# Spreading the small VectorE operations of a segment softmax between the large ones of a graph-attention loop

## The reference, cut to what matters

```python
Q, K, V = ((enh @ W + b).reshape(N, 4, 64) for W, b in ...)      # N = 3125 nodes, 4 heads
mod_k = K[src] + 0.2 * rel_w[edge_relations][:, None, :]
scores = einsum('ehd,ehd->eh', Q[dst], mod_k) / 8
seg_max = segment_max(scores, dst)
ex = exp(scores - seg_max[dst]); w = ex / segment_sum(ex, dst)[dst]
agg = segment_sum(w[:, :, None] * V[src], dst)
```

## Time and profile before

| | us |
|---|---|
| median of 3 runs | 1417.63 (1417.37 to 1419.28) |
| the profiled execution | 1413.7 |
| its span, first to last instruction | 1411.7 |
| iterations 2 to 28 of `phase_edges` | 249.44 to 898.64, 649.20 |
| iterations 29 and 30 | 898.64 to 939.32, 40.68 |
| one chunk, from the first one-hots (L735) of a step 2 to the next chunk's, 502.21 to 526.24 | 24.03 |
| mean granted TensorE clock | 0.929 |

### The profile page before, as it was taken

How to read it: one execution, slowest core, us unless ns; L and a number is a source line. 1 busy time by engine, 2 the same in 40 slices (tenths; PEclk the granted TensorE clock), 3 DMA queues, 4 the chain that set the end, 5 groups by cost and what they waited for, 6 DMA issues and landing times. The chain is left out here.

```text
span 1411.7 us, 26741 instructions
## 1 busy us (share of the span) xinstructions
PE 1120.5 (79%) x7285; PEld 865.7 (61%) x7286; DVE 968.9 (69%) x2208; ACT 824.8 (58%) x2932; POOL 739.4 (52%) x853
## 2 busy tenths in 40 slices
PE   6999746888888888888888888756676479999950
PEld 4777533666666666666666666536565269999950
DVE  7676238999999999999999999634663832112115
ACT  3444300777878787878777777852244047767730
POOL 4666267766666666666666666005321444555520
PEclk9999966899999999999999999989995689999985
DMA  8232458877777777777777777038001722222218
GB/s 230 96 119 95 107 152 253 235 225 210 217 210 213 214 209 216 207 214 209 216 208 216 211 216 213 18 119 274 19 19 56 233 75 70 67 67 67 70 38 272
DMA packets 132711, 225.07 MB, mean 159 GB/s; under 512 B 23555, under 2 KB 89098, under 8 KB 132594
## 3 DMA queue, kind: packets, MB, share of 16 engines
q0 software_dynamic: 43456, 138.49, 34.9%
q1 hardware_dynamic: 89138, 85.16, 20.0%
HBM read 191.18 MB, written 32.40 MB: 158 GB/s over the span
## 5 line engine op out<-in xcount | busy, mean ns | idle before, releaser
L568 POOL DMA_INDIRECT KV<-kv,ixs x464 | 456.9, 985 | 227.1 <-issue 115.1
L583 ACT ACTIVATE KV<-KV,WS 128x65 f32<-128x65 f32 x1856 | 469.7, 337 | 19.3 <-ACT RR L609 17.0
L669 PE MATMUL ps_o<-KV,PM 128*128 128x260 f32 x928 | 254.4, 397 | 18.7 <-DVE PM L764 8.5
L653 PE MATMUL ps_qe<-Q,PT 128*128 x1392 | 200.0, 283 | 3.9 <-DVE KV L753 3.9
L669 PEld LDWEIGHTS ps_o<-KV,PM 128*128 128x128 f32 x928 | 159.6, 192 | 64.8 <-issue 30.0
L653 PEld LDWEIGHTS ps_qe<-Q,PT 128*128 128x128 bf16 x1392 | 139.3, 101 | 53.8 <-issue 7.0
L675 PE MATMUL ps_o<-ACC,ident 128*128 x464 | 154.8, 416 | 0.0
L753 DVE TENSOR_TENSOR KV<-KV,ps_qe 128x512 f32<-128x512 f32 x232 | 147.6, 673 | 0.8 <-PE ps_qe L653 0.5
L759 DVE TENSOR_REDUCE S<-KV 128x16 f32<-128x1024 f32 x116 | 141.5, 1220 | 7.6 <-DVEq L815 0.5
L746 DVE TENSOR_TENSOR KV<-KV,ps_u 128x1024 f32<-128x1024 f32 x116 | 139.8, 1205 | 3.9 <-DMA KV<-kv,ixs 3.9
L1434 DVE TENSOR_TENSOR YG<-ps_y,B 128x256 f32<-128x256 f32 x56 | 23.8, 425 | 170.0 <-PE ps_y L1408 170.0
(11 more groups left out here) (299 smaller groups left out, 1670.8 us busy)
## 6 DMA issues: line engine op xcount, KB each, us to landing
dlb<-dl_rows SPq DMA_DIRECT2D x116, 128.0 KB
W<-in_f_W_dram SPq DMA_DIRECT2D x16, 512.0 KB, 6.0
tyb<-ty_rows SPq DMA_DIRECT2D x116, 64.0 KB
KV<-kv,ixs POOLq DMA_INDIRECT x464, 4.2
kv<-kvb SPq DMA_DIRECT2D x25, 258.0 KB, 2.6
xs_rows<-xs SPq DMA_DIRECT2D x25, 256.0 KB, 2.5
YF<-ytab SPq DMA_DIRECT2D x8, 640.0 KB, 9.2
VB<-kv SPq DMA_DIRECT2D x5, 650.0 KB, 9.0
```

Source lines behind the costliest of these rows:

```text
L568: pool.indirect_dma_start(kv[:, c % KR, n, :], None, d["kv"], bass.IndirectOffsetOnAxis(ap=T["ixs"][:, c % KR, n:n + 1], axis=0)).then_inc ...
L583: m = a.activation(part, part, ACT.Copy, scale=W[:, c % 2, s * H + h:s * H + h + 1])
L653: m = pe.matmul(T["ps_qe"][:, p % 3, k, :], T["PT"][:, h, (p % 2 * 2 + k) * P:(p % 2 * 2 + k + 1) * P], T["Q3"][:, bass.ds(at + n * C, C)] ...
L669: m = pe.matmul(T["ps_o"][:, p % 2, 0:A], PM[:, p % 2, k, :], kv[:, c % KR, 2 * x + k, C:KVW], start=(k == 0), stop=False)
```

## The change

- `softmax(c, g)` is taken apart into functions which stand at several places of the step, and `then` is gone. Each operation only counts up `s_sm`; a wait stands where a result is read. The trailing ENGINE_NOP of g = 3 goes, so `SMV` is 12 in place of 13.
- Order of a step of VectorE after: `onehots(G+1)`; g 3: `first_rows`; `modify`; g 2: `carry_in(0)`; g 3: `factors`; `place`; g 0: `run_forward`; g 2: `carry_in(1)`; `multiply`; g 2: `differences`; (last two chunks: `weigh(p + 1)`); `multiply`; g 0: `rescale`, `run_backward`; g 1: `carry`; `reduce`; g 1: `carried`.
- `place` makes the one-hots of a group in one operation, 128 x 512, in place of two of 128 x 256. `PM` has two buffers of a group. TensorE's `aggregate(p)` waits for the group's.
- For the last two chunks summed (pairs from `VP` on) the odd pair of each group is weighed by VectorE in one TENSOR_TENSOR of 128 x 2 x 4 x 65, the even one by ScalarE.
- ScalarE's `exponents` moves from the middle of step 3 to the end of step 2. TensorE's `turn_weights` moves from behind the last `aggregate` of step 3 to in front of it.

```diff
-    SMV = 13
+    SMV = 12
+    VP = (NCH - 2) * CP
+
+    def on_vector(p):
+        return p >= VP and p % 2 == 1
@@ scalar
-                        if g == 3:
-                            exponents(i - 1)
                     if i >= 2:
-                        weigh(p + 1)
+                        if not on_vector(p + 1):
+                            weigh(p + 1)
                         keep_sums(p, at[0])
                         before = at[1]
+                    if g == 2 and 1 <= i <= NCH:
+                        exponents(i - 1)
@@ tensor, aggregate
-                pe.wait_ge(s_pm, p + 1)
-                pe.wait_ge(s_wv, p + 1)
+                pe.wait_ge(s_pm, p // 2 + 1)
+                if on_vector(p):
+                    pe.wait_ge(s_wd, (p - VP) // 2 + 1)
+                else:
+                    pe.wait_ge(s_wv, p + 1 if p < VP else VP + (p - VP) // 2 + 1)
@@ tensor, loop
+                    if 1 <= i <= NCH and g == 3:
+                        turn_weights(i - 1)
                     if p >= 0:
                         aggregate(p + 1)
-                    if 1 <= i <= NCH and g == 3:
-                        turn_weights(i - 1)
@@ vector
             def place(p):
-                wait(v, s_pw, p - 1)
-                v.tensor_tensor(PM[:, p % 2, :, :], T["iota_f"][:, :].unsqueeze(1).broadcast_to([P, 2, P]),
-                                T["DC"][:, 2 * p:2 * p + 2].unsqueeze(2).broadcast_to([P, 2, P]), ALU.is_equal).then_inc(s_pm, 1)
+                wait(v, s_pw, p - 2)
+                v.tensor_tensor(PM[:, p // 2 % 2, :, :], T["iota_f"][:, :].unsqueeze(1).broadcast_to([P, G, P]),
+                                T["DC"][:, 2 * p:2 * p + G].unsqueeze(2).broadcast_to([P, G, P]), ALU.is_equal).then_inc(s_pm, 1)
+
+            def weigh(p):
+                c, x = divmod(p, CP)
+                v.wait_ge(s_w, 2 * c + 2)
+                part = kv[:, c % KR, 2 * x:2 * x + 2, C:KVW].rearrange("p s (h d) -> p s h d", h=H)
+                w = W[:, c % 2, 2 * x * H:(2 * x + 2) * H].rearrange("p (s h) -> p s h", h=H)
+                v.tensor_tensor(part, part, w.unsqueeze(3).broadcast_to([P, 2, H, D + 1]), ALU.mult).then_inc(s_wd, 1)
...
+            def run_forward(c):
+                br, et = chunk_rows(c)
+                v.wait_ge(s_bl[c % 2], 80 * (c // 2 + 1))
+                v.wait_ge(s_t1, c + 1)
+                v.tensor_tensor_scan(SF[:, :], br[:, 0, :], ps_s[0:B, 0:P], -BIG, ALU.add, ALU.max).then_inc(s_sm, 1)
+
+            def run_backward(c):
+                br, et = chunk_rows(c)
+                v.wait_ge(s_sm, c * SMV + 1)
+                wait(v, s_t2, c)
+                v.tensor_tensor_scan(SB[:, ::-1], br[:, 1, ::-1], SF[:, ::-1], -BIG, ALU.add, ALU.max).then_inc(s_sm, 1)
+
+            def carry(c):
+                br, et = chunk_rows(c)
+                v.wait_ge(s_ez, c + 1)
+                v.tensor_tensor_scan(line(ec[0:1, 0, :, :]), line(et[:, 0, :, :]), line(ez[0:1, 0, :, :]), -BIG, ALU.add, ALU.max).then_inc(s_sm, 1)
+                v.tensor_tensor_scan(line(ec[0:1, 1, :, :])[:, ::-1], line(et[:, 1, :, :])[:, ::-1], line(ez[0:1, 1, :, :])[:, ::-1], -BIG,
+                                     ALU.add, ALU.max).then_inc(s_sm, 1)
+
+            def carried(c):
+                br, et = chunk_rows(c)
+                v.wait_ge(s_sm, c * SMV + 4)
+                wait(v, s_t3, c)
+                v.tensor_copy(ez[0:1, 0, :, 0:1], ec[0:1, 0, :, CB_:CB_ + 1]).then_inc(s_sm, 1)
+                v.tensor_tensor(turned_line(cr[0:1, 0, :]), ec[0:1, 0, :, 0:CB_], et[:, 2, :, 1:CB_ + 1], ALU.add).then_inc(s_sm, 1)
+                v.tensor_tensor(turned_line(cr[0:1, 1, :]), ec[0:1, 1, :, 2:EW], et[:, 3, :, 1:CB_ + 1], ALU.add).then_inc(s_sm, 1)
+
+            def carry_in(c, n):
+                br, et = chunk_rows(c)
+                if n == 0:
                     v.wait_ge(s_t3, c + 1)
+                    v.wait_ge(s_sm, c * SMV + 7)
+                else:
+                    v.wait_ge(s_sm, c * SMV + 8)
+                v.scalar_tensor_tensor(out=SM[:, :], in0=br[:, 2 + n, :], scalar=ps_s[0:B, 256 + n:257 + n], in1=(SM if n else SB)[:, :],
+                                       op0=ALU.add, op1=ALU.max).then_inc(s_sm, 1)
+
+            def differences(c):
+                v.wait_ge(s_sm, c * SMV + 9)
+                wait(v, s_ex, c)
+                v.tensor_tensor(SD[0:H, P:P + 1], ps_s[0:H, 256:257], SM[0:H, 0:1], ALU.subtract).then_inc(s_sm, 1)
+                v.tensor_tensor(SD[:, 0:P], ps_s[0:B, 0:P], SM[:, :], ALU.subtract).then_inc(s_sm, 1)
+
+            def first_rows(c):
+                v.tensor_scalar(T["OH"][:, :], T["iota_f"][0:H, :], T["d0"][:, c:c + 1], None, ALU.is_equal).then_inc(s_sm, 1)
+
+            def factors(c):
+                v.wait_ge(s_sm, c * SMV + 12)
+                wait(v, s_t4, c)
+                v.wait_ge(s_ex, c + 1)
+                v.scalar_tensor_tensor(out=T["LR"][:, :], in0=T["OH"][:, :], scalar=T["SE"][0:H, P:P + 1], in1=T["OH"][:, :],
+                                       op0=ALU.mult, op1=ALU.subtract).then_inc(s_lr, 1)
@@ setup
-                          ... "PM": ((P, 2, 2, P), F32),
+                          ... "PM": ((P, 2, G, P), F32),
```

More of the change, by code:

```diff
@@ L517, in phase_edges @@
     s_bl = [sem(f"ed_breaks{h}") for h in range(2)]
-    (s_ix, s_oh, s_u, s_qe, s_ku, s_mu, s_sc, s_pm, s_wv, s_pw, s_o, s_acc, s_rs, s_ld) = (sem("ed_" + n) for n in
+    (s_ix, s_oh, s_u, s_qe, s_ku, s_mu, s_sc, s_pm, s_wv, s_pw, s_o, s_acc, s_rs, s_ld, s_wd) = (sem("ed_" + n) for n in
         ("indices", "onehots", "relations", "queries", "modified", "multiplied", "scores", "placements", "weighted", "placed", "products",
-         "added", "rescaled", "loads"))
+         "added", "rescaled", "loads", "weighted_by_vector"))
     (s_t1, s_t2, s_t3, s_t4, s_ez, s_sm, s_ex, s_lr, s_w) = (sem("sm_" + n) for n in
@@ L664, in aggregate @@
                 c, x = divmod(p, CP)
-                pe.wait_ge(s_pm, p + 1)
-                pe.wait_ge(s_wv, p + 1)
+                pe.wait_ge(s_pm, p // 2 + 1)
[3 more added lines that the diff above has]
+                    pe.wait_ge(s_wv, p + 1 if p < VP else VP + (p - VP) // 2 + 1)
                 wait(pe, s_acc, p - 1)
                 for k in range(2):
-                    m = pe.matmul(T["ps_o"][:, p % 2, 0:A], PM[:, p % 2, k, :], kv[:, c % KR, 2 * x + k, C:KVW], start=(k == 0), stop=False)
+                    m = pe.matmul(T["ps_o"][:, p % 2, 0:A], PM[:, p // 2 % 2, p % 2 * 2 + k, :], kv[:, c % KR, 2 * x + k, C:KVW], start=(k == 0), stop=False)
                 m.then_inc(s_pw, 1)
@@ L773, in rescale @@
                                        op0=ALU.add, op1=ALU.mult).then_inc(s_rs, 1)
[L775 to L801, removed]
-                    v.wait_ge(s_t3, c + 1)
[L803 to L815, removed]
@@ new lines, in _, with chunk_rows, line, turned_line @@
+            ez, ec, cr, SF, SB, SM, SD = (T[n] for n in ("EZ", "EC", "CR", "SF", "SB", "SM", "SD"))
+            def chunk_rows(c):
+                return T["BR"][:, c % 2, :, :], T["ET"][0:1, c % 2, :, :, :]
+            def line(t):
+                return t.rearrange("a h s -> a (h s)")
+            def turned_line(t):
+                return t.rearrange("a (s h) -> a h s", h=H)
+            def run_forward(c):
[3 more added lines that the diff above has]
+                v.tensor_tensor_scan(SF[:, :], br[:, 0, :], ps_s[0:B, 0:P], -BIG, ALU.add, ALU.max).then_inc(s_sm, 1)
@@ L821, in _ @@
                     p = (i - 2) * CP + 2 * g
+                    c = i - 1
+                    scored, softmax, summed = G_ < NG, 1 <= i <= NCH, i >= 2
                     if G_ + 1 < NG:
                         onehots(G_ + 1)
-                    if G_ < NG:
+                    if softmax and g == 3:
+                        first_rows(c)
+                    if scored:
                         modify(G_)
-                    if i >= 2:
-                        place(p)
-                        place(p + 1)
-                    if G_ < NG:
-                        multiply(2 * G_)
+                    if softmax and g == 2:
+                        carry_in(c, 0)
+                    if softmax and g == 3:
+                        factors(c)
+                    if summed:
+                        place(p)
+                    if softmax and g == 0:
+                        run_forward(c)
+                    if softmax and g == 2:
+                        carry_in(c, 1)
+                    if scored:
+                        multiply(2 * G_)
+                    if softmax and g == 2:
+                        differences(c)
+                    if summed and on_vector(p + 1):
+                        weigh(p + 1)
+                    if scored:
                         multiply(2 * G_ + 1)
-                    if i >= 2 and g == 0:
+                    if summed and g == 0:
                         rescale(i - 2)
-                    if 1 <= i <= NCH:
```

(11 more changed lines are left out.)

## The result

The changed kernel takes **1360.21 us** (median of 4, 1357.18 to 1360.95) against 1417.5 before; ratio 0.9595, 95% interval 0.9571 to 0.9618. Forecast 1357.6. The profiled execution has a span of 1359.1 against 1411.7, 52.6 less.

| stretch, us | before | after | difference | forecast |
|---|---|---|---|---|
| up to the end of iteration 1 | 249.41 | 250.43 | +1.0 | -1 |
| iterations 2 to 28 | 648.92 | 596.01 | -52.9 | -54.8 |
| iterations 29 and 30 | 40.99 | 37.97 | -3.0 | -4.2 |
| all behind | 472.4 | 474.7 | +2.3 | 0 |

A forecast was written before the change was run, and what follows sets the result against it. VectorE, 96% busy in iterations 2 to 28, was taken as the bound. 1413.7 - 54.8 (27 chunks) - 1 (iteration 1) - 4.2 (end) = 1353.7 profiled, 1357.6 against the median; own range 1350 to 1369, 8 in 10: 1349 to 1375.

The forecast's parts named there:

- The price of a wait: VectorE's softmax: a wait for the instruction just issued costs 0.11 to 0.12 us; twelve removed save 1.32 a chunk.
- The NOP's 0.22: VectorE, behind `LR`: removing the ENGINE_NOP brings `reduce` from 0.48 to 0.26 after `LR` starts, 0.22 us a chunk.
- The rule that I had priced as a rival: VectorE: next operation starts only once the pipe is empty, so spreading saves nothing; 1406 us, 3%.
- The two waits laid bare: VectorE, steps 2 and 3: `reduce` now directly follows the second `multiply` it needs; costs 0.12 each, 0.23 a chunk.
- The wait before rescale: VectorE, step 0: idle 0.42 plus lost overlap 0.08 vanishes as ScalarE's weights come earlier; 0.50 us a chunk.
- The walk: Timing from step 3's start: ScalarE's weights reach VectorE at 8.76 us, VectorE comes to `rescale` at 9.0.
- TensorE keeps up: TensorE's own chain is 20.2 us a chunk, under 22, despite new `PM` waits of 0.3 and 0.5 (steps 2, 3).
- The placement: VectorE's one-hots in one 128 x 512 instruction save 0.07 us a group, 0.28 a chunk (bounds 0 and 0.4).
- GpSimd's and the DMA engines' shares rise by 24/22: In the shorter chunk GpSimd's busy share rises to 71% and the DMA engines' to 83%; no limit expected there.
- my 22.0: Forecast length of a chunk in iterations 2 to 28, in us: 2.03 less than before.
- 0.06 not given back: VectorE's 4 x 1 and 1 x 4 operations may not overlap fully; 0.06 us a chunk was deducted from the saving.
- The last two chunks: Iterations 29 and 30: weighing on two engines (steps 4.37 to 4.1) and earlier `turn_weights` save 4.2 us together.

The follow-up runs named there:

- waits_back: Changed kernel with a wait for its own end again behind each of the 12 small softmax operations: 1394.19 us.
- before_fewer_waits: Kernel before, order kept, without 7 of its 12 waits and without the ENGINE_NOP and its wait: 1392.99 us.
- two_placements: Changed kernel with each group's one-hots made in two operations of 128 x 256 again: 1359.62 us.

## Why the prediction was right, and where it was not

The time came out by luck as well as by reasoning: the waits, the main term, were priced about rightly, the placement's term failed, and two further errors nearly cancelled.

*The price of a wait* (0.11 to 0.12, twelve of them and the NOP): shown for the twelve by waits_back and before_fewer_waits. The NOP's 0.22 was never tested alone. A wait costs a little more behind the shortest operations, 0.11 to 0.23 at L828 and L830. The rule that I had priced as a rival (the Trainium skill, "VectorE: DVE Perf Modes", section "The DRAIN you can't avoid": a semaphore after each operation costs nothing extra) would have left waits_back at 1360; it took 1394. The measurement decides. The same section also says that a next operation that is not held starts earlier, and with that the rows agree (0.26 from start to start for 0.34 long operations), so the prediction took from the page only the half that the rows speak against.

*The two waits laid bare*, 0.12 each: there, as in the earlier trace rows.

*The wait before rescale*: gone, and by the mechanism named. The walk gave 0.24 us to spare, and 0.7 of waiting was expected with `turn_weights` behind; measured 0.84.

*TensorE keeps up*: yes. The wait for `PM` at step 3 is 0.38, forecast 0.5; the 0.3 forecast at step 2 is not there. ScalarE's wait for the weights is 0.71, forecast 0.5.

*The placement*, -0.28 a chunk: the operation costs what was said, but nothing was won. Two placements a group in place of one left the time as it was (two_placements). That is the term that failed, with the sentence "GpSimd's and the DMA engines' shares rise by 24/22". The shares came to 77% and 79%, where 71% and 83% were forecast; the failure is that I had read GpSimd's 65% busy as slack. Its 0.30 of issue ahead of each gather isn't counted as busy, and its pauses for buffers had hidden that sixteen gathers need 20.1 us at 1.257 from start to start (511.48 to 512.73) and 22.07 with what it is held up. The chunk of 22.07 is GpSimd's as much as VectorE's, and the two stand in a fixed phase to each other. Without the longer `PT`, 4 x (0.450 - 0.345) = 0.42, VectorE's own would be 21.65, and with half the gathers it was 21.57. By luck my 22.0 came out all the same, because a saving 0.2 larger than I had worked out (shorter pitches of the tiny operations, 0.06 not given back) and 0.3 of longer `PT` than before nearly cancelled. The forecast was nearer than its terms deserve.

*The last two chunks*, -4.2: measured -3.0. The steps of iteration 30 didn't get to 4.1 but stayed at 4.36: the copy waits 1.51 for TensorE and 0.18 of issue is laid bare. Weighing on two engines gave 1.4 on top of the earlier `turn_weights`, at the two ends only, and nothing in the steps. The mechanism (a chain takes the place of a busy engine) was right, its price too low.

## What to carry to other kernels

A wait of an engine for its own last instruction hardly shows in the idle column (0.04 of its 0.11 to 0.12 us here); read it from start-to-start distances, and put another instruction between writer and reader. Before trusting an engine's slack, add its issue gaps to its busy time and ask what it does once its pauses are gone: here the third engine, at 65%, was the next limit. When an engine shows no wait and still doesn't get faster, compare the mean durations of its instructions before and after.

## What the runs showed of the hardware

VectorE and GpSimd hold each other up. Gathers got longer in the changed kernel (989 to 1076 ns in the mean, single ones 1.83 us) where they met a placement with two inputs in SBUF, and were 992 when one input came from PSUM, at equal length of the placement itself. `PT`, a bf16 comparison of one tensor, got longer (381 to 450 ns), by up to 0.24 us each and only where it started 0.48 to 0.69 us into a gather; it fell to 340 when GpSimd had half the gathers. As a result small shifts of VectorE's order change the time of both. This agrees with the Trainium skill ("GPSIMD Engine Reference", section 1, "Specifications": the SBUF interfaces are shared with VectorE, with contention for two SBUF inputs and for 2-port modes); that `PT` runs in such a mode is not shown by a run here. Neither lengthening appears as waiting in any view.
